# Attention and expert kernel: the first units and the last super-group laid out anew

## The reference, cut to what matters

```python
xn = layernorm(x)
# attention
qkv = silu(xn @ qkv_w.T)                      # 32 heads, q, k, v of 128 each
for blocks of 32 tokens:                      # the same as a masked product
    scores = (q @ k.T) * decay
    out = scores @ v + (q * q_decay) @ kv
xf = attn * rsqrt(mean(attn * attn) + eps) * norm_w
attention = (sigmoid(xn @ gate_w.T) * xf) @ out_w.T
# experts: 8 of rank 16, the best two of each token
logits = xn @ W_router.T
combine = softmax(logits), kept for the best two and divided by their sum
expert_out = sum over e, r of (xn @ A[e, r]) * combine[e] * B[e, :, r] * 2
ffn = xn @ W_base.T + b_base + expert_out
return x + attention + ffn
```

## Time and profile before

| what | us |
|---|---|
| median of 3 runs | 1158.83 |
| lowest and highest | 1156.89 and 1160.56 |
| the profiled execution | 1157.6 |
| its span, first to last instruction | 1155.8 |
| TensorE busy in the span | 1090.5 (94%) |
| DVE, ACT, POOL busy | 727.8, 688.8, 642.2 |

### The profile page before, as it was taken

One profiled execution on the slowest core, in us unless ns is written; L12 is line 12 of the kernel. 1 busy time (PEld: TensorE's weight loads), 2 busy tenths in 40 slices (PEclk: granted clock), 3 DMA queues, 4 the chain that ended last, 5 costly groups with the idle time before them and its releaser, 6 DMA issues. The chain is left out here.

```text
span 1155.8 us, 18941 instructions
## 1 busy us (share of the span) xinstructions
PE 1090.5 (94%) x5848; PEld 946.0 (82%) x5848; DVE 727.8 (63%) x1212; ACT 688.8 (60%) x1401; POOL 642.2 (56%) x629
## 2 busy tenths in 40 slices
PE   2669989999999999999999999999999999999985
PEld 2458878988889888988889888988889888988974
DVE  5646747566665767566656757575666757465646
ACT  5636746566566756566656756576556756575520
POOL 3644865448473765458473755457473756367420
PEclk9879999999999999999999999999999999999989
DMA  6230411111010211011020211011020211011021
GB/s 210 79 115 4 165 64 46 38 42 60 24 60 18 78 40 52 30 41 59 23 76 1 82 36 64 18 41 59 23 77 2 86 35 59 19 42 60 26 98 73
DMA packets 41973, 64.23 MB, mean 56 GB/s; under 512 B 3920, under 2 KB 21328, under 8 KB 41424
## 3 DMA queue, kind: packets, MB, share of 16 engines
q1 hardware_dynamic: 41648, 63.73, 17.2%
q10 hardware_dynamic: 288, 0.03, 0.0%
HBM read 54.84 MB, written 8.91 MB: 55 GB/s over the span
## 5 line engine op out<-in xcount | busy, mean ns | idle before, releaser
L391 POOL TENSOR_TENSOR w_lo<-combo,w_hi 128x768 fp32r<-128x768 f32 (+1 forms) x132 | 171.7, 1309 | 167.2 <-ACT w_hi L531 167.0
L391 POOL TENSOR_TENSOR w_lo<-raw,w_hi 128x256 fp32r<-128x256 f32 (+1 forms) x132 | 133.8, 1016 | 134.5 <-ACT w_hi L531 134.1
L1068 DVE TENSOR_TENSOR acc<-acc,outp 128x512 f32<-128x512 f32 x120 | 82.2, 685 | 76.4 <-PE outp L1352 75.3
L1350 PE MATMUL bank_q<-t_hi,w_hi 128*128 128x512 f32 x288 | 116.0, 403 | 10.2 <-ACT ys L531 4.7
L434 POOL TENSOR_TENSOR sum_sq<-sum_sq,square 128x512 f32<-128x512 f32 x64 | 82.9, 1296 | 73.8 <-ACT square L667 73.8
L1352 PE MATMUL bank_q<-t_hi,w_lo 128*128 128x512 f32 x288 | 113.9, 396 | 0.0
L1351 PE MATMUL bank_q<-t_lo,w_hi 128*128 128x512 f32 x288 | 113.8, 395 | 0.0
L1350 PE MATMUL outp<-wo_hi,g_hi 128*128 128x512 f32 x256 | 102.9, 402 | 9.1 <-DVE g_lo L1052 4.7
L964 DVE TENSOR_TENSOR xs<-bank_r,xs 128x512 f32<-128x512 f32 x66 | 45.6, 691 | 99.7 <-ACT xs L531 71.0
L1020 DVE TENSOR_TENSOR score<-score,table 128x512 f32<-128x512 f32 (+1 forms) x128 | 75.9, 627 | 42.4 <-PE score L1352 42.3
L1352 PE MATMUL outp<-wo_hi,g_lo 128*128 128x512 f32 x256 | 102.3, 400 | 0.0
(11 more groups left out here) (195 smaller groups left out, 3396.9 us busy)
## 6 DMA issues: line engine op xcount, KB each, us to landing
raw<-w_chunks SPq DMA_DIRECT2D x165, 256.0 KB, 2.9
table<-near_dram SPq DMA_DIRECT2D x32, 128.0 KB, 2.0
near_dram<-near_b SPq DMA_DIRECT2D x3, 1024.0 KB, 5.1
acc<-x SPq DMA_DIRECT2D x8, 256.0 KB, 6.0
acc<-x SPq DMA_DIRECT2D x2, 1024.0 KB, 6.4
xb_dram<-acc SPq DMA_DIRECT2D x2, 1024.0 KB, 5.3
y<-xb_dram SPq DMA_DIRECT2D x2, 1024.0 KB, 7.1
out<-acc SPq DMA_DIRECT2D x8, 256.0 KB, 2.1
```

Of the source, the lines that this page charges most:

```text
L391: pool.tensor_tensor(piece(w_lo[i % 2], j), piece_source(i, j), piece(w_hi[i % 2], j).bitcast(F32), ALU.subtract).then_inc(wlo[j], 1)
L1068: dve.tensor_tensor(tile, tile, outp, ALU.add).then_inc(acc_done, 1)
L1350: pe.matmul(out_, a_hi, b_hi, start=start, stop=False, skip_group_check=True)
```

## The change

The body of the six middle super-groups stays as it is, but for one pair of ACT instructions that change places (silu and copy of bank q in `V2`). Three stretches are new.

**Ahead of the first super-group.** The tokens are normalised batch by batch: mean, variance, power and refinement are done for batch 0 alone, then for batch 1. Head 0's query and key and the gates of heads 0 and 1 are no longer Strassen units but plain products, `first_rows(r, b)`: four rows r by two batches, twelve matmuls of 512 columns each, instead of two units of seven products of six. Their weights are split by POOL alone (`split_first`), their results go straight to silu and tanh, and the router products stand between them. Plain products need no combined token blocks, so the first of them wait for batch 0 only. The seven token blocks now lie in `b_hi`, `b_lo` (three plain ones, written by ACT and DVE straight from PSUM) and `c_hi`, `c_lo` (four combined ones, whose raw form lies in `acc`). The decay tables lie in `near`, under `c_hi` and `c_lo`, and are stored in two parts.

**The routing** moves into the first super-group: `two_best` and `weigh_experts` on DVE stand in place of the outputs -4 and -3, which the first super-group doesn't have, the turning of the expert rows on PE (`turn_hw`) and their copy on DVE (`keep_hw`) in place of the outputs -2 and -1. The softmax is replaced by one tanh on ACT of half the gap between the two best logits. SP stores the rows to `hw_dram` ahead of the first `xb_dram` store, and waits for them there. `output(0)` waits for `hwt_done` too.

**The last super-group** has lists of its own on PE, DVE, ACT and POOL. The scores of its last heads stand earlier. The expert rows, then the expert weights, go through `raw[0]` one after the other, ahead of the last output weights. The expert products are added into the banks of the base units (`expert` within products 2, 3 and 4) and, for result x, into `score` (`more_experts`). `y` is split by batch, each half over the q and k of its batch, and its tiles are loaded singly. Batch 1 is finished first, its last output is scaled straight out of PSUM; product 4 of `G01` comes last and batch 0 is finished behind it. The stores still go in the order of tiles 0 to 7.

```diff
 # SP
-            unit_taken(0, LAST + QK0)
+            sp.wait_ge(first_wlo, 1)
             load_v(0, 0, 1, 11, 1)
...
-            sp.wait_ge(turned, NTB)
+            sp.wait_ge(t_lo_done, 3)
+            sp.wait_ge(t3_lo_done, 1)
             sp.dma_start(base_b, ...)
             sp.dma_start(acc[:, TB:, :], x_tok[:, 0:TB, :]).then_inc(xb_in[0], 16)
-            sp.wait_ge(hwt_done, 2)
-            sp.dma_start(hw_dram, hw_t).then_inc(hw_out, 16)
...
                 load_rows(1, 20 * g + 13, 20 * g + 17)
                 if first:
+                    sp.wait_ge(hwt_done, 2)
+                    sp.dma_start(hw_dram, hw_t).then_inc(hw_out, 16)
                     sp.wait_ge(xb_done, 1)
...
+                if final:
+                    sp.wait_ge(hw_out, 16)
+                    sp.dma_start(raw[0]..., hw_dram)
+                    sp.wait_ge(hwlo_done, 1)
+                    sp.dma_start(raw[0][:, 0:2, :], w_chunks[FFN_B:FFN_B + 1]...)
+                    sp.wait_ge(btlo_done, 1)
                 load_rows(0, 20 * g + 18, 20 * g + 19)
...
             for t in range(NTB):
-                sp.wait_ge(result_done, t + 1)
+                if t < TB:
+                    sp.wait_ge(result_done, t + 1)
+                else:
+                    sp.wait_ge(last_done, t - TB + 1)
                 sp.dma_start(out_tok[:, t, :], acc[:, t, :])
 # POOL, ahead of the first super-group
+            def split_first(u):
+                pool.wait_ge(raw_in[u], 32)
+                pool.tensor_copy(first_hi[:, u], raw[u][:]).then_inc(first_whi, 1)
+                pool.wait_ge(first_whi, u + 1)
+                pool.tensor_tensor(first_lo[:, u], raw[u][:], first_hi[:, u]..., ALU.subtract)
...
+            power(1, slice(0, TB))
+            split_first(0)
+            power(2, slice(TB, NTB))
+            split_first(1)
 # PE, ahead of the first super-group
+            for t in range(TB):
+                turn_tokens(t)
+            first_rows(0, 0)
+            first_rows(1, 0)
+            first_rows(2, 0)
+            for t in range(TB, NTB):
+                turn_tokens(t)
+            first_rows(3, 0)
+            for t in range(4):
+                router(t)
+            first_rows(0, 1)
+            first_rows(1, 1)
+            for t in range(4, NTB):
+                router(t)
+            first_rows(2, 1)
+            first_rows(3, 1)
+            pe.wait_ge(t_lo_done, 3)
+            pe.wait_ge(t3_lo_done, 1)
+            pe.wait_ge(first_low, TB)
 # DVE, in the first super-group
+                early = {-4: two_best, -3: weigh_experts, -2: lambda: keep_hw(0), -1: lambda: keep_hw(1)}
 # PE, the end of the last super-group
+                    prod(G01, 1)
+                    output(10)
+                    prod(G01, 6)
+                    output(11)
+                    rms(1, 0)
+                    more_experts(0)
+                    prod(G01, 7, 5, 2, 3)
+                    more_experts(1)
+                    output(12, 13, 14, 15)
+                    rms(0, 1)
+                    prod(G01, 4)
```

More of the change, by code:

```diff
@@ L70, in unit @@
 def unit(g, i):
-    return UNITS * g + (2 + i)
+    return UNITS * g + i
 def ev(g, i):
@@ L83, in weights_in @@
 def weights_in(g, i):
[L84 to L87 removed]
+    return raw_full(g, RAW_OF[i])
+RAW_OF = {V1: 0, V2: 1, QK1: 2, QK2: 3, G23: 5, QK3: 6, QK0: 7, G01: 9, NEXT + V1: 10, NEXT + V2: 11}
 RAW_WO = (4, 8)
@@ L613, in body, with copy_m1 @@
             def body(g, first=False, final=False):
-                copy_m1, copy_u2, copy_u3, silu_, whole_, hi_, gate_, weight_ = units(g)
+                copy_m1_, copy_u2, copy_u3, silu_, whole_, hi_, gate_, weight = units(g)
+                def copy_m1(i):
+                    if first and i == V2:
+                        act.wait_ge(route, 1)
+                        act.activation(gap[:], gap[:], ACT.Tanh, scale=0.5).then_inc(route_act, 1)
+                    copy_m1_(i)
                 def silu(i, c):
-                    if not (final and i == QK0):
+                    if not (first and i < 0):
@@ L900, in _ @@
-            silu(LAST + QK0, "p")
-            whole(LAST + QK0, "p")
-            hi(LAST + QK0, "p")
-            silu(LAST + QK0, "x")
-            silu(LAST + QK0, "q")
-            whole(LAST + QK0, "q")
-            hi(LAST + QK0, "q")
-            whole(LAST + QK0, "x")
+            for t in range(3):
+                tokens_whole(t)
+            first_q(0)
+            tokens_whole(3)
+            first_k(0)
+            weight(V1, 2)
+            tokens_hi(4)
+            tokens_hi(5)
@@ L918, in _ @@
-            copy_u2(LAST + G01)
-            copy_u3(LAST + G01)
-            weight(V2, 2)
-            gate(LAST + G01, "x")
-            gate(LAST + G01, "q")
-            gate(LAST + G01, "p")
-            weight(V2, 3)
-            for t in range(2):
-                act.wait_ge(hw_turned, t + 1)
-                copy(hw_t[:, 512 * t:512 * t + 512], score[:, t, :]).then_inc(hwt_done, 1)
-            act.wait_ge(near_out, 64)
+            first_gates(0, 0)
+            weight(V2, 2)
+            act.wait_ge(near_out, 32)
@@ new lines, in inverse_root, with scaled, result @@
+                def inverse_root(b, n):
+                    refine(3 + n, slice(TB * b, TB * b + TB))
+                def scaled(t, of, more):
+                    return dve.scalar_tensor_tensor(out=acc[:, t, :], in0=of, scalar=rs[:, 1, t:t + 1], in1=more, op0=ALU.mult, op1=ALU.add)
+                def result(t):
+                    dve.wait_ge(acc_done, 16 * g + NTB + t + 1)
+                    for c in "pq":
+                        dve.wait_ge(free[c], unit(g, QK0 + t // 2) + 1)
+                    scaled(t, acc[:, t, :], y[0][:, t, :]).then_inc(result_done, 1)
@@ L1531, in _, with router @@
                 mm.then_inc(turned, 1)
+            def router(t):
+                pe.wait_ge(xt_done, max(t, TB + t // 3) + 1)
+                at = t % 3 * (ER + EXPERTS)
+                for kc in range(KC):
+                    mm = pe.matmul(routed[t // 3][:, at:at + ER + EXPERTS], x_t[:, kc, t // TB, t % TB * P:t % TB * P + P], ar[:, kc, :],
+                                   start=t % 3 == 0 and kc == 0, stop=kc == KC - 1, skip_group_check=True)
+                mm.then_inc(h_ready, 1)
```

1090 lines of the change are left out of this document (753 added, 337 removed).

## The result

The changed kernel takes 1125.45 us (median of 4 runs, 1124.05 to 1125.85) against 1158.36 us of the kernel before on the same chip: a ratio of 0.971, 95% interval 0.969 to 0.973. The forecast was 1129.5 us. Timed once more beside the experiments it gave 1124.92 us, ratio 0.971 (0.969 to 0.974). The profiled execution has a span of 1123.8 us, so 32.0 us less than the 1155.8 before.

A forecast was written before the change was run, and what follows sets the result against it. PE was taken as full in the middle, with waits only in the three rewritten stretches. Terms -25.4 - 2.0 + 2.5 + 0.9 + 7.8 - 13.1 = -29.3 gave span 1126.5, execution 1128.3, forecast 1129.5 us; range 1118 to 1141.

The forecast's parts named there:

- The start: Ahead of the first super-group: its first product comes at 55.8 instead of 81.2, 25.4 us earlier; bounds 51.5 and 62.
- I expect three pauses: PE ahead of the first super-group: 1.6 us before plain products, about 1.1 for gates' weights, 1.5 for batch 1's normalisation.
- The lower clock at the start: First super-group: PE comes straight from plain products, so 2.0 us of slow matmuls go; bounds 0 and 2.5.
- Routing: First super-group: 16 small and two larger DVE operations, 5.4 us, partly in gaps, cost 2.5 us; bounds 0 and 8.
- SP's queue: First super-group: SP's wait for `hwt_done` delays all behind it 6.3 us, plus 1.5 of lower clock: 7.8; bounds 0, 11.
- The last super-group: From its start to the end 152.5 us against 165.6, a gain of 13.1; bounds 16 and 6.
- `output(5)` waits 1.7 us: Last super-group: the chain through `raw[0]` makes the `G01` weights some 3 us later, so PE waits 1.7 us.
- (1): First super-group: the store of the expert rows is hidden, the 7.8 us go, 1121.7 us; chance 0.15.
- (2): Both new stretches: DVE and POOL stand in line, start slips to 62, routing costs 5, 1138 us; chance 0.22.
- (3): Last super-group: the chain through `raw[0]` holds it for 6 us, 1135.5 us; chance 0.10.
- (4): SP's late queue doesn't catch up, each later unit waits for weights, 1160.7 to 1165.9 us, slower; chance 0.02.
- (5): The new stretches don't act at all, the time stays at 1159 us; chance 0.01.

The follow-up runs named there:

- x3_g01: Changed kernel with SP issuing the weights of `G01` earlier in the last super-group, ahead of its wait for the split expert weights: 1121.38 us, ratio 0.968.
- the two experiments: Changed kernel without 13 small routing operations on DVE, 1120.83 us; changed kernel with the routing moved two splits and make_u2(V2) later, 1123.32 us.
- x1_sp: Changed kernel with SP storing batch 0's sum and issuing batch 1's load before it waits for the turned expert rows: 1119.46 us, ratio 0.967.
- The second profile: Changed kernel run and profiled once more, unaltered, as a yardstick: 1124.92 us, ratio 0.971, span 1121.1.
- x5_nosplit: Changed kernel with the split by batch undone, all eight tiles measured before the first is normalised: 1136.13 us, ratio 0.981.
- x9_wait: Kernel with the split by batch undone, plus POOL waiting until all eight tiles are normalised before splitting the first weights: 1129.08 us, ratio 0.974.
- x7_norm: Changed kernel with the small copy of four norm weights moved from the first super-group's gate_att(0) to behind batch 1's normalisation: 1122.59 us, ratio 0.969.

## Why the prediction came out, point by point

**The start, -25.4 predicted, -28.4 measured.** PE's work was sized right (35.3; 36.6 busy, of which some 1.4 because the first seven matmuls of 512 columns came 0.43 us from start to start instead of 0.23. That is the pace behind the pause of 4.64 us too, where the granted clock is 0.55 in the next 5 us; in this first window the clock column reads 1.00, so here only the pace speaks for the lower clock). The first tile came at 14.7, not 16.2. I had put its gain down to the four tiles less to measure, 4.1 us. The experiment without the split measured all eight and still had it at 16.8, against 20.28 before, so most of the gain lies elsewhere: DVE's four refinements took 4.2 us in the kernel before, beside POOL's weight splits, and 0.7 there. The changed kernel, with one of them held, spends 2.7 on them; unheld, its first tile would come some 2.0 us sooner by the chain, which no run has tried. POOL's copy, for which I had guessed 1.3, took 1.04. What failed is the step "I expect three pauses": the pause for batch 0's last token was 1.50 (1.6 predicted), the two others, 1.1 and 1.5, were not there. (Where PE's first products went at the full pace, as in x3_g01, the third appears with 0.44 us.) I had put POOL's second split behind a late power of batch 1; that power came at 20.30, right behind batch 0's low parts.

**The lower clock at the start, -2.0 predicted, about nothing measured.** The first product of `V1` indeed took 0.28 us instead of 0.58. But behind the routing's pause of 1.91 us the lower clock came 19 us later (0.79 in 72 to 77, above), and the granted clock of the whole stretch is 0.96 against 0.97 before. The term is given back, not absent: 120.1 - 115.5 = 4.6 us lost to the lower clock, against some 3.9 in the kernel before (118.7 busy, and an estimated 114.8 of work, 115.5 less the 0.7 us of turning below). My yardstick for that work, 113.5, was 1.3 us too low.

**Routing, +2.5 predicted**, 1.9 for its pause and up to 2.7 with the clock in the two experiments. The operations cost 0.25 us each as taken from the earlier trace rows, one of them 0.66 beside POOL.

**Turning the expert rows, +0.9 predicted**: two groups of 0.35 us, 0.7.

**SP's queue, +7.8 predicted, +6.8 measured.** Its store came 50.6 us behind the start where I had read 51 from the order. The +6.0 of the whole stretch is 4.6 us more idle time, 0.7 of turning and 0.7 more of lower clock. The terms as measured one by one, 2.7 + 0.7 + 6.8 = 10.2, are 4.2 more than that. x1_sp, which is the change without SP's wait, shows where those 4.2 are: it takes 0.8 us less than the kernel before and not 3.4 more. Its pause for `QK0`'s weights is 2.79 instead of 3.77 and one before it 0.50 instead of 0.95, 1.4 us together; the lower clock costs it 2.0 instead of 3.9, 1.9 less; and 0.8 of the routing's 2.7 was lower clock, not idle time, and is counted in the 2.0 already.

**The last super-group, -13.1 predicted, -9.2 measured.** The wait for `y` went, as forecast. PE's work of 142.0 us holds: without the pause (the `G01` experiment) the last part takes 161.6 us, and 142.0 + 3.6 + 5.2 + the 10.3 from attend to start make 161.1. The tail was 3.6 + 5.3 for 3.6 + 5.2. The mis-sized term is "`output(5)` waits 1.7 us": the right instruction, the right chain through `raw[0]`, but 2.82 us, and with about 2 us of lower clock behind it (0.83 in 1056 to 1066), which I had priced in the first super-group and forgotten here. The second profile shows how near this was: 1.65 us, and the clock at 1.00 in the same window. The bounds for the tail from the earlier trace rows, 3.8 and 6.4, have the measured 5.3 us between them. By the Trainium skill, "DMA: Bandwidth & Descriptors", section "Anatomy of one DMA", whose figures are for a GpSimd-issued DMA, I had estimated 5.0 us for these bytes; SP's five stores took 5.3, so its order of size holds for them here.

**The rivals.** (1), the store hidden, is refuted by its place and by the experiment. (2), DVE and POOL in line, is true as a mechanism, but did not cost what the rival said. Ahead of the first super-group it is on the path once, with about 2.0 us of batch 0's refinement; what is held of batch 1 is hidden behind PE's work. The small copy, held for 4.33 us inside the super-group, costs 1.0 us of pauses. Without the split by batch it would have cost 5.5 us more. (3) is half there, at 2.8 of its 6 us. (4): one pause at `QK0` and none after it; SP caught up. (5), no effect, is out with a ratio of 0.971.

The rows of the table of the result are off by -3.0, -3.2, -0.4 and +3.9 us, so part of the nearness of 1129.5 to 1125.45 is luck: the errors of opposite sign leave 2.7 us of the span. The rest of the 4.1 us is the step from one execution to the median, +1.2 forecast and -0.1 measured.

## What to carry to other kernels

Move a small store behind a wait only after asking what else stands in that queue: a wait for 0.5 MB of expert rows kept a finished 1 MB sum in the queue behind it for 10.9 us and cost about 6 us of the kernel. Place DVE's SBUF-to-SBUF work where POOL idles, and count that as a part of what an order is worth. A pause of PE has a second price, the lower clock behind it, that comes in one execution and not in the next; so take small pauses away even where their own length is under the noise. For the same reason, split a difference between two profiles into idle and busy time of PE before it is credited to an edit.

## What the runs showed of the hardware

DVE and POOL in line: four normalisations of 128x512 (one tensor operand, SBUF to SBUF) took 1.92 us alone and 7.50 beside POOL's two copies and two subtractions; a refinement of 4 elements 0.90 beside a copy of 1.03; another 2.20 us beside a subtraction of 2.34; a gate of 128x512 with an operand in PSUM 0.70 us beside a bias add of 4.80. The Trainium skill, "SBUF — State Buffer", section "SBUF: two separate sides", says that the shared pair of ports is held for the whole instruction, and that of DVE's operations those in a two-port mode or with two inputs in SBUF contend for it. The trace agrees: the first three were held, and the gate, with one input in SBUF, was not. x5_nosplit and x9_wait show what it is worth. One row is different: beside POOL's two powers (2.00 us together, 4 elements each) the refinements took 0.16 to 0.17 us in x5_nosplit and x9_wait, as if alone; why these did not hold DVE is open, the more so as POOL's times are rough.

The clock around a pause: behind the pause of 1.50 to 1.67 us ahead of the first plain product, the first matmul took 0.76 us in the changed kernel and 0.47 in x3_g01 and x7_norm, which change nothing before it; the tiles turned ahead of that pause went at the slower pace in both (1.94 us for eight, 1.04 later), so in the one PE was still slow and in the other it had just become fast. Behind the pause of 1.91 us the granted clock of the next 5 us was 0.79 in one and 1.00 in the other (x3_g01). In x3_g01 the two together are worth 2.3 us of the span, as much as one of the edits above brings.
